# Running the MLP tiles six steps behind the attention chunks, with the weight chunks dequantised inside the attention steps

## What is computed

```
x = x + attention(layernorm(x), Wq, bq, Wk, bk, Wv, bv, Wbeta, bbeta, Walpha, balpha)
x = x + mlp(layernorm(x), gate, up, down)
```

## Time and profile before

| | |
|---|---|
| median of 3 runs | 1163.4 us (1162.24 to 1163.8) |
| the profiled execution, its own time | 1162.27 us |
| its span from first to last instruction | 1160.5 us |
| granted TensorE clock | 1.0 of full speed |
| PE busy | 1149.0 us, 99% |
| DVE, POOL, ACT busy | 718.2, 505.6, 432.3 us |
| DMA | 41.93 MB, mean 36 GB/s |

### The profile page before, as it was taken

The page is one execution under the profiler, slowest core; times in us unless marked ns, Lnnn a source line. Parts: engine busy times, 40 slices in busy tenths (PEclk is TensorE's granted clock), DMA queues, the critical chain, the costliest instruction groups (busy, mean ns, idle before and its releaser), DMA issues.

```text
span 1160.5 us, 19350 instructions
## 1 busy us (share of the span) xinstructions
PE 1149.0 (99%) x7793; PEld 762.1 (66%) x7793; DVE 718.2 (62%) x1239; ACT 432.3 (37%) x979; POOL 505.6 (44%) x503
## 2 busy tenths in 40 slices
PE   9899999999999999999999999999999999999998
PEld 5566555566544445777777777777777777777775
DVE  7887554565666764665666566656665666555333
ACT  4343432344133232334434344434343434343332
POOL 2376332335255754335634463446353635363110
PEclk9999999999999999999999999999999999999999
DMA  8021110000010010110011001100110011000011
GB/s 298 21 84 28 32 33 10 19 19 19 8 66 1 19 37 19 37 37 19 19 37 37 19 19 38 38 19 19 37 38 19 20 37 37 19 22 26 37 38 64
DMA packets 22681, 41.93 MB, mean 36 GB/s; under 512 B 2688, under 2 KB 2752, under 8 KB 22592
## 3 DMA queue, kind: packets, MB, share of 16 engines
q1 hardware_dynamic: 22592, 40.70, 11.0%
HBM read 36.46 MB, written 4.23 MB: 35 GB/s over the span
## 4 chain that ended last, share of the span: by engine, by line
PE 96%; DVE 2%; POOL 1%; ACT 0%; issue 0%; POOLq 0%; DVEq 0%; ACTq 0%
PE ps L467 38%; PE ps L501 29%; PE ps L428 14%; PE ps L333 9%; PE ps L387 1%; PE ps L301 1%; PE ps L370 1%; PE ps L394 1%; PE ps L381 1%; PE ps L508 1%; PE ps L361 1%; POOL WR L1252 0%; DVE wf L1013 0%; DVE XT L836 0%; DVE bigA L830 0%
## 5 line engine op out<-in xcount | busy, mean ns | idle before, releaser
L501 PE MATMUL ps<-WR,ihl_s 128*128 128x512 f16 x768 | 183.6, 379 | 0.0
L501 PE MATMUL ps<-WR,vv 128*128 128x512 f16 x720 | 172.5, 379 | 0.0
L428 PE MATMUL ps<-XT,WR 128*128 128x512 f16 x768 | 170.4, 379 | 0.0
L467 PE MATMUL ps<-XT,WR 128*128 128x256 f16 x1152 | 157.1, 273 | 0.0
L467 PE MATMUL ps<-REG,WR 128*128 128x256 f16 x1152 | 157.1, 273 | 0.0
L1029 DVE TENSOR_TENSOR load<-load,ps 128x256 f32<-128x256 f32 x144 | 60.7, 421 | 144.3 <-PE ps L467 93.2
L467 PEld LDWEIGHTS ps<-REG,WR 128*128 128x128 f16 x1152 | 112.7, 98 | 33.5
L428 PEld LDWEIGHTS ps<-XT,WR 128*128 128x128 f16 x768 | 75.0, 98 | 90.3 <-DVE fw L955 0.9
L724 ACT COPY load<-ps 128x256 f32<-128x256 f32 x144 | 53.7, 373 | 211.1 <-PE ps L467 211.1
L1252 POOL TENSOR_TENSOR WR<-wf,WR 128x512 f16<-128x512 f32 x48 | 57.8, 1224 | 149.6 <-ACT WR L674 149.6
L467 PEld LDWEIGHTS ps<-XT,WR 128*128 128x128 f16 x1152 | 112.7, 98 | 13.3
(11 more groups left out here) (165 smaller groups left out, 1812.4 us busy)
## 6 DMA issues: line engine op xcount, KB each, us to landing
load<-codes SPq DMA_DIRECT2D x48, 256.0 KB
load<-scales SPq DMA_DIRECT2D x48, 256.0 KB
y<-X SPq DMA_DIRECT2D x16, 256.0 KB, 2.0
bigA<-cla SPq DMA_DIRECT2D x14, 256.0 KB, 3.2
X<-x SPq DMA_DIRECT2D x3, 1024.0 KB, 14.0
WR<-wqkv SPq DMA_DIRECT2D x2, 1024.0 KB, 10.1
X<-x SPq DMA_DIRECT2D x4, 256.0 KB, 3.9
WR<-wqkv SPq DMA_DIRECT2D x4, 256.0 KB, 4.4
```

What stands on the lines that cost most here:

```text
L428: mm = eng.matmul(bank[:, :], buf[:, wp, o + kt, 128 * j:128 * j + 128], XT[:, xp, kt, 512 * b:512 * b + 512], start=(n == 0), stop=(n == 11))
L467: mm = eng.matmul(half_bank(kind, name), w(wp, kt), x(xp, kt), start=(first and n == 0), stop=(n == 5), skip_group_check=True)
L501: mm = eng.matmul(PS[bank][:, :], ih[:, ip, 128 * tt:128 * tt + 128], buf[:, wp, 8 + j, :], start=(j == 0 and p == 0), stop=(j == end and ...
```

## The change

The MLP tiles run six steps behind the attention (`APART = 6`), so that upgate(0 to 9) are in the loop, 10 and 11 behind it. No chunk is dequantised in stage 1 any more. Chunks 0 to 6 belong to the steps T = 1, 3, 4, 5, 8, 9, 13. Chunks 0 and 1 have dq_bits at the end of steps 0 and 2 and dq_finish before `weigh` of steps 1 and 3; for the others dq_bits and dq_finish lie in one step, behind `weigh` and `apply`, on either side of the projections. The downs of n = 0 move from step 8 to 10, those of n = 1 from steps 12 to 15 (one each) to 14 and 15 (two each), those of n = 2 behind upgate(12). In every step with an upgate it now precedes the turn and mid. The turn of tile 15 comes right behind upgate(11). SP issues two chunk loads ahead of the loop in place of four.

```diff
-DEQUANTED = (0, 1, 5, 7, 13)
+DEQUANTED = (1, 3, 4, 5, 8, 9, 13)
+APART = 6
...
-            return (PS[2], PS[3]) if i < 12 or i % 2 else (PS[4], PS[5])
+            return (PS[4], PS[5]) if i > 10 and i % 2 else (PS[2], PS[3])
...
@@ PE, upgate(i) @@
-                if i == 12:
+                if i == 11:
                     pe.wait_ge(s_attn, NT)
                     for sm5, value in banks.freed[5]:
                         pe.wait_ge(sm5, value)
-                elif i == 13:
-                    pe.wait_ge(s_inter, 12)
                 elif i >= 12:
                     pe.wait_ge(s_inter, i - 1)
@@ PE, the loop @@
-                i, fill = T - 4, fills(T)
+                i, fill = T - APART, fills(T)
...
-                if T == 8:
+                if T == 10:
                     for tt in range(4):
                         down(0, tt)
-                if T >= 12:
-                    down(1, T - 12)
-                if i > 0 and i % 4:
+                if T >= 14:
+                    down(1, 2 * T - 28)
+                    down(1, 2 * T - 27)
+                if i >= 0:
                     upgate(i)
                     turn("n2", T - 1)
                     mid(T)
-                elif i >= 0:
-                    turn("n2", T - 1)
-                    mid(T)
-                    upgate(i)
...
-            for tt in range(3):
-                down(2, tt)
-            turn("n2", NT - 1)
-            down(2, 3)
             banks.ring = [0, 1, 6, 7]
-            for i in range(12, 32):
+            for i in range(NT - APART, 32):
                 upgate(i)
+                if i == 11:
+                    turn("n2", NT - 1)
+                if i == 12:
+                    for tt in range(4):
+                        down(2, tt)
@@ ACT @@
-                if T == 12:
-                    dequant(0)
...
-            dequant(1)
...
-                if T >= 4 and T % 4 == 0:
-                    turn("n2", T - 1)
-                if T >= 4:
-                    act_tile(T - 4)
-                if T % 4:
+                if T >= APART:
+                    act_tile(T - APART)
+                if T >= 1:
                     turn("n2", T - 1)
                 if T in DEQUANTED:
                     dequant(dk)
                     dk += 1
+            act_tile(NT - APART)
+            act_tile(NT - APART + 1)
             turn("n2", NT - 1)
@@ DVE @@
-                if T == 9:
-                    dq_bits(0)
-                elif T == 11:
-                    dq_finish(0)
-                elif T == NT - 1:
-                    dq_bits(1)
...
-            dq_finish(1)
...
-            dq_bits(2)
...
                 weigh_keys(T)
-                if T in DEQUANTED:
+                if T in (1, 3):
                     dq_finish(dk)
                     dk += 1
                 weigh(T)
                 if T >= 1:
                     apply("n2", T - 1)
+                if T >= 4 and T in DEQUANTED:
+                    dq_bits(dk)
                 for f in fill:
                     project(*f)
+                if T >= 4 and T in DEQUANTED:
+                    dq_finish(dk)
+                    dk += 1
...
+                if i >= 0:
                     act_tile(i)
                     turn_low("n2", T - 1)
                     mid(T)
...
-                if T in (0, 1, 5, 9):
+                if T in (0, 2):
                     dq_bits(dk)
             apply("n2", NT - 1)
...
+            act_tile(NT - APART)
+            act_tile(NT - APART + 1)
             turn_low("n2", NT - 1)
-            gather(2, 3)
@@ POOL @@
-                if T == NT - 3:
-                    dequant(0)
-            dequant(1)
...
@@ SP @@
             load_chunk(1)
-            load_chunk(2)
-            load_chunk(3)
```

More of the change, by code:

```diff
@@ L747, in _ @@
             project("q", 1, 1)
-            dk = 2
+            dk = 0
             for T in range(NT):
@@ L1083, in _ @@
                     apply("n2", T - 1)
+                if T >= 4 and T in DEQUANTED:
+                    dq_bits(dk)
                 for f in fill:
                     project(*f)
-                if T == 8:
+                if T >= 4 and T in DEQUANTED:
+                    dq_finish(dk)
+                    dk += 1
+                if T == 10:
                     for tt in range(4):
                         gather(0, tt)
-                if T >= 12:
-                    gather(1, T - 12)
-                if i > 0 and i % 4:
+                if T >= 14:
+                    gather(1, 2 * T - 28)
+                    gather(1, 2 * T - 27)
+                if i >= 0:
                     act_tile(i)
@@ L1094, in _ @@
                     mid(T)
[L1095 to L1098, removed]
                 else:
@@ L1102, in _ @@
                         turn_low("n2", T - 1)
-                if T in (0, 1, 5, 9):
+                if T in (0, 2):
                     dq_bits(dk)
             apply("n2", NT - 1)
-            for tt in range(3):
-                gather(2, tt)
+            act_tile(NT - APART)
+            act_tile(NT - APART + 1)
             turn_low("n2", NT - 1)
-            gather(2, 3)
             dq_bits(7)
@@ L1116, in _ @@
                 if i == 12:
+                    for tt in range(4):
+                        gather(2, tt)
                     dq_finish(8)
@@ L1332, in _ @@
                     decay_rows(T + 2)
-                if T >= 4:
-                    inter_low(T - 4)
+                if T >= APART:
+                    inter_low(T - APART)
                 if T in DEQUANTED:
@@ L1338, in _ @@
             norm_scale("n2", NT - 1)
+            inter_low(NT - APART)
+            inter_low(NT - APART + 1)
             dequant(7)
@@ L1421, in _ @@
             load_rows(3)
-            k = 4
+            k = 2
             for T in range(NT):
```

## The result

The changed kernel is **slower**: median 1170.39 us (1169.21 to 1171.0, 4 runs) against 1163.38 us, a ratio of 1.0063 with a 95% interval of 1.0051 to 1.0076. The forecast was 1166.7 us, +3.3 us; measured are +7.0. The time lies inside the range of 1161.8 to 1170.5 by 0.1 us, on the forecast's side of the sign, but the size is off by a factor of two. That the difference of the medians is that of the two profiled executions is in part luck: each median lies 1.1 to 1.2 us above its profiled execution.

What follows compares the result with a forecast made beforehand. The prediction took PE to bound the kernel except in stage 1, where it waits for DVE. New stalls of 8.9 us less gains of 5.6 made +3.3 on 1163.4: 1166.7 us, range 1161.8 to 1170.5.

Steps and rivals of the forecast that it cites:

- stage 1: Before the loop: PE's three transpose waits for DVE go, gain 4.4 us (3.5 to 4.8).
- the price of a chunk: On DVE: bits 2.12 us alone, 3.5 beside POOL; finish 1.2 alone, 1.52 and 2.57 beside POOL.
- steps 4 and 5: Attention loop: a whole chunk on DVE delays the k evictions PE needs; stalls of 2.0 us for both (0.9 to 3.6).
- step 0: Attention loop: bits and finish of chunk 2 leave this step, gain 0.7 us (0.2 to 0.7).
- step 2: Attention loop: the bits beside POOL's chain go, the head's delay stays; gain 0.5 us (0 to 0.8).
- step 3, stall: Attention loop: bits(1) and finish(1) ahead of weigh(3) on DVE stall PE 2.2 us (1.7 to 4.4).
- step 14: First down there waits for turn_low(12), delayed by chunk 6 on DVE in step 13: 2.2 us (1.7 to 3.6).
- ahead of upgate(12): End of the loop: upgate(12) waits for tile 15's low half, no down covering it: 2.5 us (2.3 to 2.7).
- the slack of 1.6 us: Step 3: spare DVE time before PE wants weigh's result, set against 3.3 to 6.0 us of new work.
- DVE's work stays hidden: Rival: in steps 3, 4, 5 and 13 no stalls, only the loop's end costs; -3.1 us, 1160.3 us, chance 0.12.
- The low ends: Rival: chunk operations at lone speed, gains in full; 6.6 less 6.0, +0.6, 1164.0 us, chance 0.30.
- DVE and POOL hold each other up: Rival: bits and finish slowed beside POOL in all places; +8.5 us, 1171.9 us, chance 0.10.

Runs made afterwards that it cites:

- the filler: Changed kernel with 30 idle transposes into an unused bank in PE's wait of step 3: 1168.02 us.
- t45_evict_first: Changed kernel with the bits of chunks 2 and 3 behind the projections' evictions in steps 4 and 5: 1169.0 us.
- end_downs_first: Changed kernel with the four downs of n = 2 between the turn of tile 15 and upgate(12), their gathers ahead of chunk 7 on DVE: 1167.31 us.
- t13_split: Changed kernel with the bits of chunk 6 at the end of step 12 and its finish behind turn_low(12) in step 13: 1168.38 us.
- stage1_back: Changed kernel with chunks 0 and 1 and their loads in stage 1 again, none in steps 0 to 3: 1169.39 us.
- t3_finish_behind: Changed kernel with only the finish of chunk 1 moved behind weigh of step 3: 1167.21 us.
- t3_pool_waits: Changed kernel with POOL's mask and subtraction for the next steps held in step 3 until weigh(3) is done: 1169.1 us.

## Why the prediction was wrong in size

The places were right, all of them. Three things failed: the price of a chunk in step 3 (1.5 us too low), that in steps 4 and 5 (0.9 too low), and a term put at nothing, TensorE's lower clock behind a stall (1.6 us). Point by point, counted from start to start on PE, predicted and measured in the profile:

```
                                     predicted     measured
stage 1                               -4.4          -4.2
gates                                  0            -0.4
step 0                                -0.7          -0.7
step 2                                -0.5          -0.5
start of the run                       0            -0.3
step 3, stall                         +2.2          +3.7
step 3, half clock behind it           0            +1.6
steps 4 and 5                         +2.0          +2.9
step 14                               +2.2          +2.3
ahead of upgate(12)                   +2.5          +2.6
sum (of the unrounded terms)          +3.3          +6.9
```

- **Stage 1** came as worked out: the three waits went, and turns 10 and 14 are left 0.3 us late each, where the text said up to 0.3. The gates' wait for ACT became 0.4 us shorter (0.66 to 0.30 from start to start); I had them at nothing, and what shortened it I didn't test.
- **Step 3, the stall** is the first step that failed. "bits 2.4, finish 1.4: nearer to the low end, since POOL is done with its longest operations while much of it runs" was wrong on both. They took 2.9 and 2.4; put into the same sum, less the slack of 1.6 us, they give the 3.7 that was measured. I had read the earlier trace rows, where finish had taken 2.57, and gave that price to a rival of chance 0.10, which puts it in all places. It was nearly the right one for finish(1), since there too each of its two multiplications met a POOL operation. They were not the same operations, though, as the prediction has it: in step 0 of before they were the decay's product and the mask, in step 3 of the changed kernel the mask and the subtraction. The lines of before:

```profile
73.95 1.12 DVE L1013 SCALAR_TENSOR_TENSOR wf<-tb,load 128x512 f32<-128x512 f16 x1
```

```profile
72.44 1.04 POOL L1226 TENSOR_TENSOR bigB<-bigB,kn_s 128x512 f32<-128x512 f32 x1 [0.49 <-POOL kn_s L1223]
73.44 1.09 POOL L1209 TENSOR_SCALAR_AFFINE_SELECT bigB<-bigB 128x512 f32<-128x512 f32 x1
```

The first multiplication, from 72.50, and the second end at 74.03 and 75.07, 0.55 us behind these two. The finish of 1.52 us, which the prediction takes as a sign that not each operation is held, fits as well: its first multiplication (0.92 us) ends 0.55 us behind POOL's L1226, and the second (0.68) met none. In step 13 finish took its lone 1.29 and bits 3.0, and the 2.3 us there fit the forecast.
- **Steps 4 and 5**: the k evictions were late by 1.4 and 1.3 us where I had taken 2.0 for both. In both, L975 took 1.52 us, held by POOL's subtraction (in step 4: POOL's 113.03, DVE's 113.27), and finish ran alone. So one held operation, 0.8 us above its lone time, is what each of these steps brings; the forecast had gone nearer to none.

```profile
113.03 1.21 POOL L1192 TENSOR_TENSOR bigA<-bigA,bigD 128x512 f32<-128x512 f32 x1
```

```profile
113.27 1.52 DVE L975 SCALAR_TENSOR_TENSOR load<-load 128x512 int32<-128x512 int32 x1
```

- **The clock** is the term that was missing altogether. The prediction counted only the length of each stall. Behind the 3.5 us without work in step 3 PE ran at half clock in each of the four profiles that have this wait, which cost 1.6 us in the changed kernel's; with the filler in the wait it didn't. Behind the stalls of 2.3 to 2.6 us it may, for 1.7 us more. The changed kernel's other three runs have a granted clock of 0.997 against 0.999 in the profiled one, and are 0.7 to 1.8 us longer. That this is the second fall is what the profiles of the other runs suggest; these three themselves have no trace.
- **Step 14 and the end of the loop** were right, by the rows of before: what a copy of the new order would cost was there to be read in step 15 of the old.
- **The rivals**: "DVE's work stays hidden" is refuted for this order, since PE waits for DVE in five new places. "The low ends" is refuted too: the gains came out in full, 6.1 us with the start, but the new stalls were 13.1 in place of 6.6 (its 6.0 of gains is also not the 6.3 of the prediction's own bounds). "DVE and POOL hold each other up" is right about the mechanism, wrong about everywhere.

## What to carry to other kernels

When an engine's work is moved into a loop that is bound by another engine, its total doesn't matter but its place does: put it behind everything the bound engine is waiting for in that step (here the weighing, the evictions that free the ring's banks, the low half of a transpose), and follow the ring of banks one turn further, since a stall that is removed at one bank can come back at the next. Price an operation by the rows in which the same neighbours run beside it, not by its lone time. And add to a stall of TensorE like these, of 2.1 us idle and more, the matmuls that may run at half clock behind it; where such a wait can't be removed, cheap matmuls into an unused bank may keep the clock, as they did in both experiments with such filler.

## What I had not expected of the hardware

Waits of TensorE of 3.5 us idle were followed by a granted clock of 0.5 in every profile that has one without filler (the changed kernel, t45_evict_first, end_downs_first, t13_split), worth 1.6 us in the changed kernel's. With 2.1 to 2.4 us idle it was so in some executions and not in others of nearly the same kernel: once in stage 1 (stage1_back), three times behind the wait of the downs of step 14 (t3_finish_behind, stage1_back, t45_evict_first) and twice behind that of upgate(12) (t13_split, t3_pool_waits), 1.7 us each time; the changed kernel's own profile has both of the last two waits and no fall behind them. The kernel before has such a wait too, and its two groups of times, 1162.1 and 1163.4 us, come together at 1162.2 when the wait is filled.

The second thing is how exactly the POOL operation sets the end of a held DVE operation: 0.55 us behind it at each place read, while DVE's operation appears in the trace as one long busy stretch. So a DVE duration well above the lone one, beside a POOL operation, was a wait here, not work.
